# Bringing the experts' first-layer weights by a transfer from SBUF to SBUF instead of a copy on VectorE

## The reference

```python
probs = jax.nn.softmax(h @ wg, axis=-1)
topv, topi = jax.lax.top_k(probs, K)                 # K = 2 of E = 8 experts
topv = topv / topv.sum(-1, keepdims=True)
w = (topv[..., None] * jax.nn.one_hot(topi, E, dtype=h.dtype)).sum(-2)
h1 = jax.nn.gelu(jnp.einsum('bsd,edf->ebsf', h, w1) + bb1[:, None, None, :])   # D = 128, F = 512
y = jnp.einsum('ebsf,efd->ebsd', h1, w2) + bb2[:, None, None, :]
moe = jnp.einsum('ebsd,bse->bsd', y, w)
return layernorm(h + moe, g2, b2)
```

## Time and profile before

| | before |
|---|---|
| median of 3 runs | 1063.59 us |
| the profiled execution | 1061.42 us |
| its span, first to last instruction | 1059.6 us |
| mean granted TensorE clock | 0.937 |
| PE, PEld busy | 902.4 us (85%), 698.3 us (66%) |
| VectorE, ACT, POOL busy | 849.5 us (80%), 769.8 us (73%), 535.0 us (50%) |

### The profile page before, as it was taken

One profiled execution on the slowest core, in us unless ns is written; L12 is line 12 of the kernel. 1 busy time (PEld: TensorE's weight loads), 2 busy tenths in 40 slices (PEclk: granted clock), 3 DMA queues, 4 the chain that ended last, 5 costly groups with the idle time before them and its releaser, 6 DMA issues. The chain is left out here.

```text
span 1059.6 us, 26142 instructions
## 1 busy us (share of the span) xinstructions
PE 902.4 (85%) x6922; PEld 698.3 (66%) x6922; DVE 849.5 (80%) x2533; ACT 769.8 (73%) x1905; POOL 535.0 (50%) x781
## 2 busy tenths in 40 slices
PE   1446899999999999999999998846999999999474
PEld 0234667676766766766676666536999999999421
DVE  4667989999999999998989888673777777777378
ACT  2776799999999999997897766751656656666356
POOL 8000243344356556656577767782555656656400
PEclk9657999999999999998999999965999999999788
DMA  1015543444354454545344556153333332332186
GB/s 52 1 51 130 132 108 108 113 118 111 90 136 118 120 128 118 136 108 124 104 127 126 137 140 160 40 119 102 88 99 86 92 89 85 95 86 67 48 247 190
DMA packets 138118, 114.69 MB, mean 108 GB/s; under 512 B 19459, under 2 KB 126601, under 8 KB 138005
## 3 DMA queue, kind: packets, MB, share of 16 engines
q1 hardware_dynamic: 120916, 92.24, 33.9%
q0 software_dynamic: 8640, 16.93, 5.0%
q10 hardware_dynamic: 8448, 4.20, 1.4%
HBM read 60.60 MB, written 52.58 MB: 107 GB/s over the span
## 5 line engine op out<-in xcount | busy, mean ns | idle before, releaser
L621 POOL TENSOR_SCALAR_AFFINE_SELECT b_PT<-b_PT 128x256 f32<-128x256 f32 (+1 forms) x384 | 191.0, 512 | 207.2 <-ACT b_PT L811 202.1
L1180 DVE TENSOR_REDUCE b_m_neg<-b_ps_m 128x2 f32<-128x512 f32 (+1 forms) x384 | 255.1, 681 | 33.9 <-PE b_ps_m L1615 15.8
L811 ACT ACTIVATE b_PT<-b_ps_s 128x512 f32<-128x512 f32 x384 | 219.6, 598 | 28.3 <-PE b_ps_s L1591 13.9
L1923 POOL DMA_INDIRECT results<-e_Y,e_X x142 | 151.7, 1068 | 121.4 <-DVE e_Y L1991 98.5
L656 POOL DMA_INDIRECT slots<-c_pay,b_pos x128 | 130.3, 1018 | 39.9 <-issue 36.5
L2039 PE MATMUL e_ps_d<-e_h,e_w 128*128 128x256 f32 x568 | 134.5, 380 | 0.0
L1615 PE MATMUL b_ps_m<-c_QK 128*128 128x256 f32 x512 | 123.3, 322 | 0.0
L1594 PE MATMUL b_ps_s<-c_QK 128*128 128x512 f32 x256 | 111.0, 434 | 5.6 <-ACT b_PT L811 5.4
L1950 ACT ACTIVATE e_h<-e_ps,e_w 128x256 f32<-128x256 f32 x284 | 111.3, 480 | 0.8 <-PE e_ps L2030 0.8
L2039 PEld LDWEIGHTS e_ps_d<-e_h,e_w 128*128 128x128 f32 x568 | 102.6, 191 | 11.0
L1943 ACT ACTIVATE e_yt<-e_ps_d,e_w 128x256 f32<-128x256 f32 x71 | 33.7, 475 | 99.2 <-PE e_ps_d L2039 99.2
(11 more groups left out here) (253 smaller groups left out, 2311.6 us busy)
## 6 DMA issues: line engine op xcount, KB each, us to landing
c_QK<-qk_scr SPq DMA_DIRECT2D x128, 192.0 KB
qk_scr<-b_qk_hi SPq DMA_DIRECT2D x64, 256.0 KB
e_X<-slots SPq DMA_DIRECT2D x71, 130.0 KB, 2.3
qk_scr<-b_qk_lo SPq DMA_DIRECT2D x32, 256.0 KB
f_G<-results SPq DMA_DIRECT2D x32, 256.0 KB, 3.6
a_X<-in_L_attn_x_dram SPq DMA_DIRECT2D x16, 256.0 KB, 6.4
x<-a_X SPq DMA_DIRECT2D x16, 256.0 KB, 2.8
b_X<-x SPq DMA_DIRECT2D x32, 128.0 KB, 5.7
```

Of the source, the lines that this page charges most:

```text
L621: nc.gpsimd.affine_select(out=tri, in_=tri, compare_op=ALU.is_ge, fill=0.0, base=0, pattern=[[0, tri.shape[1]], [1, P]], channel_multiplie ...
L811: nc.scalar.activation(PT[:, g % 2, q % 3], ps_s[:, q % 2], ACT.Exp, scale=HD ** -0.5).then_inc(s_e, 1)
L1180: nc.vector.tensor_reduce(out, scores, AX.X, ALU.max, negate=True).then_inc(s_red, 1)
L1923: nc.gpsimd.indirect_dma_start(dram["results"][:, :], bass.IndirectOffsetOnAxis(X[:, j.of(NB_X), u, D:D + 1].bitcast(u32), 0), Y[:, n, u, ...
```

## The change

The copy of w1 leaves VectorE; the copy of w2 stays. Instead SP issues a transfer from `kept["w1"]` to one of four buffers. For this it loads the slot's expert from `tile_e`, waits until the up matmuls of slot s-4 are done (from slot 4 on) and issues. In the written-out steps 1 to 4 the transfer for slot s-1 stands between the issue of X(s) and that of x1(s); from step 8 on the transfer for slot s-4 stands at the head of the step, ahead of X(s); those of the last four slots stand behind all steps. PE waits for one more semaphore before a slot's first up matmul, one semaphore for each buffer.

```diff
-        w1 = sb("e_w1", [P, 2, 2, F], f32r)
+        w1 = sb("e_w1", [P, 4, 2, F], f32r)
...
+        s_w1d = [sem(f"e_w1d{k}") for k in range(4)]
...
+            def weights_up(s):
+                e = expert(sync, s)
+                if s.i is not None or s.base >= 4:
+                    need_apart(sync, (s_go, 1), (s_up, (s - 4) * NF + NF))
+                sync.dma_start(w1[:, s.of(4)].bitcast(fp32), kept["w1"][:, bass.ds(e, 1)].rearrange("p e h f -> p (e h) f").bitcast(fp32)).then_inc(s_w1d[s.of(4)], 16)
+
             def step(s):
+                if s.i is not None or s.base >= 8:
+                    weights_up(s - 4)
                 n = s.of(NB_X)
...
                 sync.dma_start(X[:, n], in_t[bass.ds(at, 1)].rearrange("t p u d -> p (t u) d")).then_inc(s_x[n], 16)
+                if s.i is None and 1 <= s.base < 5:
+                    weights_up(s - 1)
                 if s.exists(NTILE):
...
             steps(sync, SLOTS, 0, NB_X, step, 8)
+            for s in range(SLOTS - 4, SLOTS):
+                weights_up(Count(s))
...
-                nc.vector.tensor_copy(w1[:, n].rearrange("p h f -> p (h f)"), kept["w1"][:, bass.ds(e, 1)].rearrange("p e h f -> p (e h f)").bitcast(fp32))
                 nc.vector.tensor_copy(w2[:, n], kept["w2"][:, bass.ds(e, 1), :].rearrange("p e f -> p (e f)")).then_inc(s_w, 1)
...
                     need(pe, s_w, s + 1)
+                    need(pe, s_w1d[s.of(4)], s.turn(4) * 16 + 16)
...
-                        nc.tensor.matmul(out, w1[:, n, 1, col], x_hi[:, n], start=True, stop=False)
-                        nc.tensor.matmul(out, w1[:, n, 0, col], x_lo[:, n], start=False, stop=False)
-                        nc.tensor.matmul(out, w1[:, n, 0, col], x_hi[:, n], start=False, stop=True).then_inc(s_up, 1)
+                        nc.tensor.matmul(out, w1[:, s.of(4), 1, col], x_hi[:, n], start=True, stop=False)
+                        nc.tensor.matmul(out, w1[:, s.of(4), 0, col], x_lo[:, n], start=False, stop=False)
+                        nc.tensor.matmul(out, w1[:, s.of(4), 0, col], x_hi[:, n], start=False, stop=True).then_inc(s_up, 1)
```

## The result

The changed kernel takes 1076.13 us (median of 4 runs, 1070.75 to 1078.14) where the kernel before takes 1062.32 (4 runs, 1059.24 to 1064.22): a ratio of 1.0125, 95% interval 1.0078 to 1.0172. A later comparison of the same two on another chip gave 1.0076 [1.0049, 1.0103], 1070.91 us over 12 runs against 1061.22 over 29. Both intervals lie above 1: by these two ratios the change makes the kernel 8 to 13 us slower. The forecast had the sign, with 1067.9, but the first result lies 1.1 us above its range.

The account below looks back on a forecast made before the run. The prediction took PE to bound the experts' stage at 3.59 us a slot. Late start 2.2, slot 5 0.8 and two late places 1.3 summed to 4.3 us, added to 1063.6 for a median of 1067.9; range 1063.5 to 1075.

Parts of the forecast that it names:

- Removal of the copies: Experts' stage: taking 71 casts of 0.70 us off VectorE, 49 us of busy time, gains 0, as PE sets the pace.
- Start: Stage's start: slot 0's weights land 3.2 us after 734.69, so the first up matmul comes at 737.9, not 735.70: +2.2 us.
- data term: Landing of a weight transfer: 524 KB at about q0's 361 GB/s take 1.45 us, besides 1.76 us fixed.
- The weights of slots 1 to 4 are issued 2.86 us apart: Start-up steps on SP: these transfers are issued faster than slots go, so they cost 0.
- Clock: Slot 0 ran at 1.2 GHz; a later start may have more or less of that, 0.6 us either way.
- (a): Slot 5: its weights, issued behind X(8), land 20.0 us after the first up matmul, due at 19.2: +0.8 us.
- (b): Behind late X(17), and one more place like it, X(13), the next weights miss their slot by 0.65 us: +1.3 in all.
- The loop's step: SP's step in the loop: about 2.0 us now plus 1.4 new, together 3.4 of a slot's 3.59 us.
- PE's third wait: Before a slot's first matmul: costs 0, at most 0.1 us a slot; as a rival, 1075 us, chance 0.05.
- traffic beside PE: PE's reads beside the new writes into SBUF: cost 0, since the casts wrote the same bytes to the same place.
- steady slots in time by 0.7: Loop: slot 33's weights land at 854.8 and the slot begins at 855.52, so they are in time by 0.7 us.
- The Trainium skill's floor: SP's value loads: about 600 ns each would make its step 4.0 us, the kernel some 28 us slower; the prediction used 278 ns.

## Why the prediction was wrong

**Removal of the copies, 0: right for the slots.** PE's pace of 3.59 us a slot stood, and the kernel without copy or transfer takes 2 us less by its ratio, which can't be told from none. What the sum did not have is the third stage, 1.0 us shorter in the profile.

**Start, 2.2: right** (2.25), though by the distance, not the time of day. From the issue at 740.18 to the matmul it took 3.30, and the landing of 3.17 was the 3.2 of the sum. Its data term came out as well: on one chip half the size landed in 2.33 to 2.47 us and the whole in 3.08 to 3.18, thus 262 KB more in 0.72 us, or about 360 GB/s, the 361 of the earlier trace rows. The 435 GB/s that the Trainium skill's page DMA: Bandwidth & Descriptors, section Bandwidth, gives for SBUF to SBUF were not reached.

**"The weights of slots 1 to 4 are issued 2.86 us apart ... faster than slots go: 0": this is the step that failed.** It failed twice. First, the spacing was taken for the answer, and the last of the four was not dated. Slot 4's transfer does not stand 2.86 behind slot 3's but behind three more steps of SP, at the head of step 8. With the prediction's own numbers, from 734.69, three times 2.86 lead to 743.27, the rest of step 4 and three plain steps of 1.65 to 749.2, load and wait to 750.3: 12.4 us after the first up matmul at 737.9. Slot 4 was due 4.8 + 3 x 3.59 = 15.6 after it, less 3.2 for the landing, 12.4 as well. The cover was 0.0 us, and it was written down as plenty. Second, the terms were too small. SP's queue, start and length of each issue (L1907 weights, L1917 X, L1922 x1):

```profile
740.18 0.60 SPq L1907 DMA_DIRECT2D e_w<-c_w1s  x1
740.82 0.58 SPq L1922 DMA_DIRECT2D c_x<-x  x1
742.74 0.41 SPq L1917 DMA_DIRECT2D e_X<-slots  x1
743.87 0.53 SPq L1907 DMA_DIRECT2D e_w<-c_w1s  x1
...
751.10 0.50 SPq L1907 DMA_DIRECT2D e_w<-c_w1s  x1
...
755.36 1.24 SPq L1917 DMA_DIRECT2D e_X<-slots  x1
...
760.17 0.50 SPq L1907 DMA_DIRECT2D e_w<-c_w1s  x1
```

The transfers are 3.69, 3.63 and 3.60 us apart. Of the 0.8 that each has over 2.86, 0.1 is the longer issue of x1 (0.58, not 0.47), 0.1 that of the weights (0.50 to 0.60, not 0.45), and 0.6 is the value load between x1 and X, which runs while the transfer's data move. (The first transfer's packets of 4 KB start between 741.43 and 742.83, and the load runs from 741.45 to 742.30.)

```profile
L1913 SPq TENSOR_LOAD <-c_tile_at x71: 264/272/866, 736.6 to 985.9; - x71
```

Its median is that of the earlier trace rows and its longest 866 ns; the long ones are the ones behind a transfer and x1. From 751.10 to 760.17 it is 9.07 instead of 7.0, with one more such load, one issue of X of 1.24 us, 0.8 too long, beside an instruction fetch, and 0.6 of small terms. All in all the issue came 16.7 us after the first matmul instead of 12.4. Slot 4, due 16.0 after it (slot 0 took 5.25), got its weights at 19.7 and began at 19.9: 3.9 late, and 5.5 of the 11.5 us with the clock behind it, where the sum had 0.

**Clock, 0.6 either way: too small, since the wait before slot 4 was not seen.** After it the clock was low for 3.4 us, 1.56 us of the loss. On the first and third chips it was not low anywhere in the slots behind the first in the kernels without a wait of that length there. A single long wait is not the only way, though: on the slow chip it was low for 3.4 us at 824.2, 930.0 and 988.0 in the kernel with half of the transfer, where no single wait of PE in the slots was over 1.9 us.

**(a), slot 5 late by 0.8: replaced** by slot 4. Slot 5's weights left SP at 763.81, 3.64 us after slot 4's, and were no longer late by themselves: one long wait had moved all the rest back. Where the start is mended and the lead is not (VectorE copies the first four), (a) comes true, behind X(8) as it was described: slot 5 is late by 1.6 us, twice the 0.8.

**(b), two places, 1.3: right in kind, short in size.** Slots 8 to 14, 60 and 64 cost 3.3. The mechanism of (b), X late in SP's queue and the next weights behind it, is there three times: X(12), X(64) and X(68) waited 2.1, 2.3 and 2.2 us for the results of slots 4, 56 and 60, and behind them the transfers of slots 9, 61 and 65 were issued 6.4, 4.7 and 4.6 us after the one before. That X(12) was late is the stall before slot 4 once more, eight slots on: both profiles of the changed kernel have it, with 2.08 us, and in the kernel with more lead X(12) did not wait. X(64) waited 3.3 us in before as well, where 1.2 to 1.9 are usual: a place that the prediction did not list. On top come instruction fetches: beside an issue of x1 of 1.24 us (778.16, ahead of slot 9's transfer), and beside landings of 3.9 (slot 13, from 795.25) and 5.0 us (slot 65, from 982.47). In before, too, such fetches stand at 765.6 and 780.3, ahead of the two late X of (b), at 768.19 and 782.57; that they made them late is not shown. The loop's step, foretold as 3.4, was 3.3 to 3.5 us, and that is why lateness heals slowly there, by 0.1 to 0.3 a slot.

**PE's third wait 0, traffic beside PE 0, steady slots in time by 0.7: right.** The window of 840 to 890 shows it; from slot 20 to slot 59 the landings are 0.6 to 1.5 us ahead of use.

**The Trainium skill's floor** of about 600 ns for such a value load (the same page, section Latency and other measured facts) would have given 28 us. It was 0.27 us with nothing beside it and 0.58 to 0.87 beside a transfer's data, so as a floor it does not hold here, but the row of before, taken where no such data moved, was no bound either.

In terms of the sum: 2.2 + 0.8 + 1.3 against 2.25 + 0.4 + 5.5 + 3.3 = 11.5 in the first profile, less the 1.0 of the third stage, and against 9.4 in the second (2.2 and 7.2), less 1.2. The medians' differences are 13.8 and 9.7 us. The 3.3 that the first has over its profile's 10.5 are within the interval of its four runs (8 to 18 us), and no step here explains them.

## What to carry to other kernels

When a copy is replaced by a queued transfer, date every transfer of the start-up by adding the whole queue in order, up to the first one that stands in the steady pattern, and set each date against its due time; a spacing says nothing of the one that stands behind the gap. A lead that is only as long as the landing makes each irregularity a stall, and a stall of some microseconds can cost clock on top. And if the engine that is relieved waits for the one that sets the pace, as here, even a perfect version brings nothing that its time can tell. Last, look at what an engine named in a view of waits was doing: in one kernel here it was the next slot's copy that ended in the wait, and the late transfer was not named.

## What the runs showed of the hardware

- A value load on SP took 0.27 us alone and 0.86 to 0.87 when it began with the data of a 512 KB transfer from SBUF to SBUF. In the kernel without x1 the load right behind the issue, ahead of the data, took 0.27, and one in the data 0.58 to 0.61.
- Such a transfer landed after 2.98 us in the median, and one of half the size 0.72 us sooner at the stage's start; the issue of either took 0.50 us on SP, and 0.60 for the first.
- Beside a fetch of 16 KB of instructions, issues on SP took up to 1.24 us instead of 0.4 or 0.47, and landings 3.9 to 5.4 instead of 3.0, with one of the 16 counts late and the others in time.
- After a wait of 3.5 to 3.6 us on PE the granted clock was at 1.2 GHz for 3.4 us, in both profiles of the changed kernel on the first and third chips.
- On one chip of three, register operations on SP took up to 0.72 us instead of 0.05; the kernel before lost 3% there, and the changed one 4% more.
